# Weights turned by a DMA transpose as f16 halves instead of by f32 transposes on TensorE, in a two-layer gated attention and FFN kernel

## What is computed

```
x = x + tanh(g_xattn[0]) * L0_xattn(layernorm(x), ctx)      # linear attention, 16 heads, gate, Wq Wg Wkv Wo
x = x + tanh(g_ffn[0])   * L0_ffn(layernorm(x))             # gelu(x proj1' + b1) proj2' + b2, 512 -> 2048 -> 512
x = x + tanh(g_xattn[1]) * L1_xattn(layernorm(x), ctx)      # softmax attention over 64 context rows
x = x + tanh(g_ffn[1])   * L1_ffn(layernorm(x))             # 8 merged experts, silu(gate) * up, down, top-8 router
```

## Time and profile before

| | us |
|---|---|
| median of 3 runs (1937.81 to 1941.26) | 1939.32 |
| the profiled execution | 1941.13 |
| its span in the profile | 1939.3 |
| PE busy, 10102 matmuls and transposes | 1900.6 |
| DVE busy | 1035.4 |
| ACT busy | 559.7 |
| POOL busy | 280.7 |
| q1, the queue of SP's loads and stores | 85.36 MB in 55922 packets |

### The profile page before, as it was taken

One profiled execution on the slowest core, in us unless ns is written; L12 is line 12 of the kernel. 1 busy time (PEld: TensorE's weight loads), 2 busy tenths in 40 slices (PEclk: granted clock), 3 DMA queues, 4 the chain that ended last, 5 costly groups with the idle time before them and its releaser, 6 DMA issues.

```text
span 1939.3 us, 25583 instructions
## 1 busy us (share of the span) xinstructions
PE 1900.6 (98%) x10102; PEld 962.7 (50%) x10102; DVE 1035.4 (53%) x2260; ACT 559.7 (29%) x873; POOL 280.7 (14%) x277
## 2 busy tenths in 40 slices
PE   6999998999999999999999999999999999999999
PEld 4556555644444444444444444444544444444444
DVE  7688866764545453443535545554555555545422
ACT  3145423422222221112212233232222333333321
POOL 3023211111102010101100011111111111111111
PEclk9999998999999999999999999999999999999999
DMA  6013322220101111110101020101010101000000
GB/s 218 12 42 124 106 89 82 87 98 17 44 28 60 28 64 50 56 55 22 62 1 55 1 71 1 50 1 50 1 50 1 50 1 45 5 11 13 1 22 22
DMA packets 56041, 86.99 MB, mean 45 GB/s; under 512 B 9042, under 2 KB 17362, under 8 KB 55922
## 3 DMA queue, kind: packets, MB, share of 16 engines
q1 hardware_dynamic: 55922, 85.36, 13.8%
HBM read 60.17 MB, written 25.17 MB: 44 GB/s over the span
## 4 chain that ended last, share of the span: by engine, by line
PE 86%; issue 8%; DVE 3%; POOL 1%; DMA 1%; ACT 1%; POOLq 0%; SPq 0%; DVEq 0%
PE bank L835 44%; PE bank L939 16%; PE bank L1033 10%; PE bank L844 5%; PE bank L919 4%; PE bank L885 1%; PE bank L904 1%; POOL arena L802 1%; PE bank L1020 1%; PE bank L968 1%; PE bank L995 0%; DMA x_after_ffn<-arena 0%; PE bank L984 0%; PE bank L983 0%; DMA arena<-x_after_attention 0%
## 5 line engine op out<-in xcount | busy, mean ns | idle before, releaser
L835 PE MATMUL bank<-arena 128*128 128x512 f16 x4608 | 1043.4, 380 | 3.1 <-DVE arena L1286 2.3
L835 PEld LDWEIGHTS bank<-arena 128*128 128x128 f16 x4608 | 451.0, 98 | 522.7 <-issue 5.5
L939 PE MATMUL bank<-arena 128*128 128x512 f16 x1536 | 352.1, 379 | 1.2 <-DVE arena L1469 1.2
L1033 PE MATMUL bank<-arena 128*128 128x512 f16 x1152 | 264.3, 379 | 0.9 <-POOL arena L802 0.9
L1621 DVE SCALAR_TENSOR_TENSOR arena<-bank,arena 128x512 f32<-128x512 f32 x96 | 72.0, 750 | 332.1 <-PE bank L835 332.1
L939 PEld LDWEIGHTS bank<-arena 128*128 128x128 f16 x1536 | 150.1, 98 | 173.9 <-DVE arena L1469 1.7
L1467 DVE TENSOR_SCALAR arena<-arena 128x512 f16<-128x512 f32 x128 | 69.4, 543 | 305.4 <-ACT arena L1134 305.2
L1134 ACT ACTIVATE arena<-bank,arena 128x512 f32<-128x512 f32 x128 | 99.6, 778 | 457.3 <-PE bank L835 454.3
L802 POOL TENSOR_TENSOR arena<-arena 128x512 f16<-128x512 f32 x96 | 111.1, 1157 | 628.7 <-ACT arena L1171 628.7
L844 PE MATMUL bank<-arena 128*128 128x128 f32 x1012 | 150.1, 279 | 26.4 <-DVE arena L1234 14.1
L1033 PEld LDWEIGHTS bank<-arena 128*128 128x128 f16 x1152 | 112.1, 98 | 128.3 <-POOL arena L802 1.4
(11 more groups left out here) (173 smaller groups left out, 1221.9 us busy)
## 6 DMA issues: line engine op xcount, KB each, us to landing
arena<-in_L_ffn_proj SPq DMA_DIRECT2D x48, 256.0 KB, 2.9
x_after_attention<-arena SPq DMA_DIRECT2D x8, 1024.0 KB, 4.7
arena<-x_after_attention SPq DMA_DIRECT2D x8, 1024.0 KB, 5.6
x_after_ffn<-arena SPq DMA_DIRECT2D x8, 1024.0 KB, 4.5
arena<-x_after_ffn SPq DMA_DIRECT2D x8, 1024.0 KB, 6.2
arena<-in_x SPq DMA_DIRECT2D x7, 1024.0 KB, 5.4
out<-arena SPq DMA_DIRECT2D x7, 1024.0 KB, 4.2
arena<-in_L_ffn_down_proj SPq DMA_DIRECT2D x48, 96.0 KB, 2.0
```

The lines of the kernel that those rows point to most:

```text
L835: m = e.matmul(bank[b][:, :], wT[l][:, c, tile * P:(tile + 1) * P], y[h][:, c, :], start=n == 0, stop=n == NPASS - 1)
L939: m = e.matmul(bank[t][:, :], hv[h][:, 0, t * P:(t + 1) * P], w2T[l][:, j, :], start=j == 0 and i == 0, stop=j == NH - 1 and i == 2)
L1033: m = e.matmul(bank[t][:, :], hv[h][:, 0, t * P:(t + 1) * P], dnT[l][:, j, :], start=j == 0 and i == 0, stop=j == NR - 1 and i == 2)
```

## The change

The tile is no longer turned on PE. ACT makes the scaled high half from the staged tile as it lies (`wsplit`), DVE the low half, both side by side in one of three new buffers `wsp` (128 x 1024 f16). A DMA transpose of the 256 KB, issued from SP, writes both into the matrix; the layout in memory becomes hi and lo chunks of a tile next to each other (`both`, `in_fours`), so that one transfer serves both halves. Three semaphores, one for each buffer, count the transposes; ACT waits for the transpose of three groups before. SP's loads wait for DVE's low half instead of PE's transpose. POOL's scaling goes away: the factor is folded into the exponent chain on DVE. The staging load of the router's zero padding, the squares and the waits of the matmuls are adapted.

```diff
@@ second(w) and weights(upto), in make_plan
         add("wlo", w)
+        add("wturn", w)
...
             if GROUPS[w][0] != "max":
-                add("wturn", w, banks=1)
+                add("wsplit", w)
                 late.append(lambda: second(w))
@@ build
-    arena = stack.enter_context(nc.sbuf_tensor("arena", [P, 207 * KB], F32))
+    arena = stack.enter_context(nc.sbuf_tensor("arena", [P, 213 * KB], F32))
+    def both(kb, k, n):
+        return at(kb, k * n, F16).rearrange("p (a n) -> p a n", a=2 * k)
+    def in_fours(kb, k, n):
+        return at(kb, k * n, F16).rearrange("p (g a n) -> p g a n", g=k // 4, a=8)
+    wsp = [at(207 + 2 * i, D, F16) for i in range(3)]
     def w_dst(name, t):
-        hi, lo = wT_of[name]
+        v = wT_of[name]
         if name == "2":
-            a, n = 4 * (t % 4), slice((t // 4) * P, (t // 4 + 1) * P)
-            return hi[:, a:a + 4, n], lo[:, a:a + 4, n]
+            return v[:, t % 4, :, (t // 4) * P:(t // 4 + 1) * P]
...
-        n = slice(t * P, (t + 1) * P)
-        return hi[:, :, n], lo[:, :, n]
+        return v[:, :, t * P:(t + 1) * P]
+    n_turned = {name: nth["wturn", i] for i, (how, name, t) in enumerate(GROUPS) if how != "max" and t == SIZE[name] - 1}
+    def w_ready(w, name):
+        for i in range(len(wsp)):
+            w.wait_ge(w_turned[i], 16 * ((n_turned[name] - 1 - i) // len(wsp) + 1))
@@ sync_program
                     else:
-                        w.wait_ge(w_turned, nth["wturn", k - 4])
+                        w.wait_ge(w_lo, nth["wlo", k - 4])
...
+            elif kind == "wturn":
+                _, name, t = GROUPS[step[1]]
+                i = (nth[step] - 1) % len(wsp)
+                src = wsp[i][0:NE, :] if name == "gw" else wsp[i]
+                w.wait_ge(w_lo, nth[step])
+                e.dma_start(w_dst(name, t), src, transpose=True).then_inc(w_turned[i], 16)
@@ pool_program
-            elif kind == "wmax" and GROUPS[step[1]][0] == "row":
...
-                w.wait_ge(w_rec, n_row)
-                e.tensor_scalar(stg[k % 4], stg[k % 4], wrec[:, c], W_TOP, ALU.mult, ALU.mult).then_inc(w_scaled)
@@ tensor_program (and the like for g, o, 1, 2, gate, up, d, gw)
-            elif kind == "wturn":
...
-                turn4(step, stg[k % 4], w_turned)
             elif kind == "q":
                 w.wait_ge(y_lo, y_rank(("A", b)))
-                w.wait_ge(w_lo, n_lo["q"])
+                w_ready(w, "q")
@@ scalar_program
-            elif kind == "wturn":
+            elif kind == "wsplit":
...
-                w.wait_ge(w_turned, n)
...
+                i, m = (n - 1) % len(wsp), (n - 1) // len(wsp)
+                if m:
+                    w.wait_ge(w_turned[i], 16 * m)
+                e.activation(wsp[i][:, 0:D], stg[k % 4], ACT.Copy, scale=scale).then_inc(w_hi)
...
-                e.activation(hi, block4(bank_of[step, 0])[:, :, 0:hi.shape[2]], ACT.Copy, scale=scale).then_inc(w_hi)
+                    e.activation(junk, stg[k % 4], ACT.Square, scale=scale, accum_out=wsq[:, c]).then_inc(w_sq)
@@ vector_program
-                    e.tensor_scalar(wpow[:, c], wpow[:, c], TINY, None, ALU.max).then_inc(w_chain)
+                    e.tensor_scalar(wpow[:, c], wpow[:, c], TINY, 1.0 / W_TOP, ALU.max, ALU.mult).then_inc(w_chain)
...
-                    e.tensor_tensor(lo, src, hi, ALU.subtract).then_inc(w_lo)
+                e.scalar_tensor_tensor(out=wsp[i][:, D:2 * D], in0=stg[k % 4],
+                                       scalar=wrec[:, c] if how == "row" else sc["s" + name], in1=wsp[i][:, 0:D],
+                                       op0=ALU.mult, op1=ALU.subtract).then_inc(w_lo)
```

More of the change, by code:

```diff
@@ L461, in build @@
     domt = small(NG, I32)
-    gwT = [small(NC * NE // 2, F16).rearrange("p (c s) -> p c s", c=NC) for _ in range(2)]
+    gw_both = small(NC * NE, F16).rearrange("p (a s) -> p a s", a=2 * NC)
+    gwT = [gw_both[:, NC * i:NC * (i + 1), :] for i in range(2)]
     bank = [stack.enter_context(nc.psum_tensor(f"bank{i}", [P, 512], F32)) for i in range(8)]
@@ L498, in build @@
     y_turned, y_hi, y_lo = sem("y_turned"), sem("y_hi"), sem("y_lo")
-    w_chain, w_rec, w_mx, w_zero, w_scaled = (sem(n) for n in ("w_chain", "w_rec", "w_mx", "w_zero", "w_scaled"))
-    w_turned, w_sq, w_hi, w_lo = sem("w_turned"), sem("w_sq"), sem("w_hi"), sem("w_lo")
+    w_chain, w_rec, w_mx, w_zero = (sem(n) for n in ("w_chain", "w_rec", "w_mx", "w_zero"))
+    w_turned = [sem(f"w_turned{i}") for i in range(len(wsp))]
+    w_sq, w_hi, w_lo = sem("w_sq"), sem("w_hi"), sem("w_lo")
     s_chain, all_in, all_out, half_in, half_out = (sem(n) for n in ("s_chain", "all_in", "all_out", "half_in", "half_out"))
@@ L527, in w_nth, with n_rows @@
         return nth[kind, w]
[L529 to L532, removed]
+    n_turned = {name: nth["wturn", i] for i, (how, name, t) in enumerate(GROUPS) if how != "max" and t == SIZE[name] - 1}
+    def w_ready(w, name):
+        for i in range(len(wsp)):
+            w.wait_ge(w_turned[i], 16 * ((n_turned[name] - 1 - i) // len(wsp) + 1))
+    def n_rows(k):
+        return sum(g[0] == "row" for g in GROUPS[:k + 1])
     def freed(step, i):
@@ L938, in tensor_program @@
                     for i, (h, l) in enumerate(PASSES):
[L939 removed]
+                        m = e.matmul(bank[t][:, :], hv[h][:, 0, t * P:(t + 1) * P], w2T[:, j // 4, 4 * l + j % 4, :],
                                      start=j == 0 and i == 0, stop=j == NH - 1 and i == 2)
@@ L1007, in tensor_program @@
                 _, b, j = step
-                w.wait_ge(w_lo, n_lo["gate"])
+                w_ready(w, "gate")
                 w.wait_ge(y_lo, y_rank(("M", b)))
@@ L1072, in scalar_program @@
                 e.activation(tanhg, gains, ACT.Tanh).then_inc(tanh_ok)
-            elif kind == "wturn":
+            elif kind == "wsplit":
                 k = step[1]
                 how, name, t = GROUPS[k]
+                c = slice(COL0[name] + t, COL0[name] + t + 1)
+                if how == "row":
+                    w.wait_ge(w_rec, n_rows(k))
+                    scale = wrec[:, c]
+                else:
+                    w.wait_ge(w_in[k % 4], w_landed[k])
+                    w.wait_ge(scale_of[name], 1)
+                    scale = sc["s" + name]
+                i, m = (n - 1) % len(wsp), (n - 1) // len(wsp)
+                if m:
+                    w.wait_ge(w_turned[i], 16 * m)
+                e.activation(wsp[i][:, 0:D], stg[k % 4], ACT.Copy, scale=scale).then_inc(w_hi)
                 if name in SQUARED:
-                    c = slice(COL0[name] + t, COL0[name] + t + 1)
-                    w.wait_ge(w_scaled, sum(g[0] == "row" for g in GROUPS[:k + 1]))
                     if n_sq:
```

61 lines of the change are left out of this document (23 added, 38 removed).

## The result

The changed kernel takes **1955.1 us** (median of 4 runs, 1954.0 to 1955.8) against 1938.7 us for the kernel before: ratio 1.0082, 95% interval 1.0066 to 1.0098. It is 16 us slower, where I had forecast 12 us faster. Its profiled execution took 1954.51 us, with a span of 1952.7 us.

What follows compares the result with a forecast made beforehand. PE, 98% busy, was taken as the bound. For the profiled execution 1941.1 - 34 (transposes) + 19.6 (start) + 2 (stalls) = 1928.7 us, less 1.8 for the median: 1927 us; range 1908 to 2040, the forecast's own 1918 to 1940.

Steps and rivals of the forecast that it cites:

- The start: q's DMA transposes queue on SP behind small loads and 3 MB of kv and context, delaying all PE work: +19.6 us.
- Rival 1: DMA transposes don't keep pace in the attention stage: 1994 us at 8 us each, 2081 at 10.5; chance 0.30.
- 77 x 0.44 = 34 us leave the path: On PE, all transpose groups except q's four, 0.44 us each, come off the time: 34 us.
- The price of a group in PE's stream: Four f32 transposes on PE cost 0.44 us, read from matmul starts with and without them.
- PE runs almost back to back after 100 us: After 100 us PE hardly waits, so its removed work was expected to shorten the result.
- DVE has 47% of the span idle: DVE's dearer low halves, at most 11 us, are hidden by its idle time from 100 us on: costed at nothing.
- I take 2 us for it: Transposes queued behind x's stores and loads on SP exceed the buffers' 16 us, stalling ACT and then PE: 2 us.
- a weight tile is wanted one step of its kind later (5 us), which hides it: SP's weight loads come some 3 us later, with stores and x loads behind them, but 5 us of slack hides this.
- My upper end: Upper bound on stalls from SP standing still, through ACT to PE: 10 us.
- Rival 3: The gain is eaten: start costs 25 us, SP's standing still costs ACT 8; 1938 us, no change; chance 0.10.

Runs made afterwards that it cites:

- experiment 1: Changed kernel with the small loads, kv and context loads and constants' step moved behind q's four groups: 1944.5 us, ratio 1.0026.
- experiment 9: Changed kernel with q's four groups turned on PE as before: 1934.2 us; second kernel, also attention-stage x ahead of weight steps on SP: 1928.7 us.
- experiment 5: Changed kernel with q's transposes and attention-stage x moved ahead on SP, plus four idle PE transposes in each of 81 groups: 1955.8 us, ratio 1.0084.
- experiment 2: Changed kernel with the attention stage's x stores and loads ahead of weight steps on SP: 1946.0 us, ratio 1.0031.
- experiment 8: Kernel before, all transposes on PE, with only SP's weight loads waiting for DVE's low half instead of PE's turn: 1949.0 us, ratio 1.005.
- experiment 7: Changed kernel with q's transposes first and x ahead of weight steps on SP in attention and first FFN: 1940.6 us; low halves also on POOL: 1945.6.
- experiment 4: Changed kernel with 80 of 81 DMA transposes replaced by plain copies in 256-byte pieces, weights not transposed: 1954.8 us, ratio 1.0078.

## Why the prediction was wrong

**Right.** The start: +18.5 us at the first q projection where I took 19.6, by the steps as they were written (small loads, then 3 MB, then the last two transposes). Experiments 1 and 9 bear it out. The last transpose was issued at 33.30 us and not at 28.8 (30.5 less its own 1.7), since the issue of the one before took 6.91; this changed little, because what it waited for, the 3 MB, landed at about 36 us where I had 38. Rival 1 did not happen: a transpose takes 1.23 us of SP (I took 1.7), 1.5 us of the engines (I took 3) and lands after 3.5 us, far under the 8 of that rival. The Trainium skill's VectorE: DVE Perf Modes (the three transpose paths), which spoke against the change, gives 1309 ns for one block by DMA. Eight blocks in 3.5 us are 440 ns each, so as a price per block of a larger transfer the trace does not agree with it.

**The step that failed first** is "77 x 0.44 = 34 us leave the path". The price of a group in PE's stream was right, but that PE's stream is the path for all 34 us was read from its share over the whole span, 98% busy. By experiment 5 the groups are worth 0.14 us each in the attention stage and 0.31 in the first FFN. The eight early ones (g and o) brought nothing that shows: the stretch from q to the first output projection is 110.3 us against 109.8. That makes 4.6 + 11.5 = 16.1 us, 18 less than forecast; by the medians of experiment 5 it is up to 18.8, and 15 less. The rows of PE back to back show it filled by those transposes; they do not show how soon the next wait comes. That PE runs almost back to back after 100 us was itself too much said: in the kernel before it waits 13.2 us in the attention stage. The same kind of average stands behind "DVE has 47% of the span idle": in that stage DVE is busy for 215.4 of 289.5 us, 74%.

**The second** is "I take 2 us for it" on SP standing still, with the sentence before it, that "a weight tile is wanted one step of its kind later (5 us), which hides it". I asked who waits for the weight tile. Late were the stores and loads of x behind it in the same queue: 8.6 us in the attention stage (experiment 2) and about 4.5 in the first FFN (experiment 8), 13 us where I took 2. My upper end was 10. Buffers and ACT's split, to which I gave that paragraph, cost next to nothing: ACT waited 2.8 us in all for the transposes.

**The sum again** with what was measured, for the profiled execution: 1941.1 + 19 (start, at the first output projection) - 16.1 + 13 = 1957.0 against 1954.5 us. The 2.5 us left are not assigned; the terms come from separate kernels and overlap. A part of both failures is the clock: PE's busy time fell by 24.3 us where 81 x 0.44 = 36 went. Most of what is missing is missing in the attention stage (6.4 in place of 14 us, at a granted clock of 0.97 against 0.98), and one reason that the rows show is that after some of the new gaps the next matmuls take longer (4.32 in place of 2.75 us for twelve, as one case). The granted clock of the whole span is 0.991 against 0.994. How much of the missing 12 us is due to it was not worked out.

**Rival 3**, the gain eaten, named the right kind of mechanism but at ACT and with 8 us, and ended at no change.

**By stage, what is settled and what is open.** Settled: the start, the late x loads, the worth of PE's transposes, that the transposes are cheap. Open: what sets DVE's results in the attention stage once PE is faster, and how to order one queue so that x and weights both come in time in the FFN (experiment 7 failed). A second queue for x was not tried, nor was x first in the kernel before; without that run it is open how much of the 10.8 us of experiment 9 needs the DMA transposes (its first kernel, with no order changed, has 5.3).

## What to carry to other kernels

A busy share of 98% says that an engine is the bound with its present work; how much of a removed piece comes out at the end has to be read from the slack of the next engine at that place, or measured by putting idle work of the same size back. When a wait in an in-order queue is changed to a later event, list what stands behind it in that queue, above all stores and loads of data that others want at once; one changed semaphore cost 9.5 us here with no other edit. When work moves from an engine to a DMA queue, leave on the engine the few pieces at the start that nothing hides: four of the 81 groups made 21 us.

## What was unexpected of the hardware

- The issue of a transpose takes 1.23 us of SP in the median, but 6.91 and 2.94 us right behind the 3 MB of kv weights and context, and 1.37 and 1.24 us when those are issued after it (experiment 1). It is not a matter of transposes: with plain copies the same wait falls on the plain load behind, 6.34 us (experiment 4).
- A transposing transfer of 256 KB inside SBUF and a plain one in 256-byte pieces land after the same 3.5 us; the plain one costs SP 0.60 us.
- After a gap of 2.21 us (experiment 8) and one of 3.52 us (the changed kernel) in a dense stretch of PE, twelve matmuls take 4.44 and 4.32 us in place of 2.75, so that the gap costs 1.6 to 1.7 us beyond its length. This does not follow every gap: after 2.45 us at 601.49 us in the second kernel of experiment 9 and 3.03 us at 711.37 in that of experiment 5, twelve take 2.75. The window of time from 682 to 775 us of experiment 8's kernel shows the granted clock at 0.98, those around it 1.00:

```profile
595.00:682.00 87.00, 87.00 (x429) 42.57 (x428) 43.66 (x96) 23.81 (x44) 11.65 (x12) 1.00 0.15 49
682.00:775.00 93.00, 90.79 (x427) 42.56 (x426) 43.02 (x83) 18.23 (x29) 8.53 (x8) 0.98 0.15 46
```

(The columns are the window, its length, busy us and instructions of PE, PEld, DVE, ACT and POOL, the granted clock, DMA's share and GB/s.)
